# Attention scores as unsplit float32 blocks of 16 rows, four at a time, with two masked buffers

## The chip, the cores and the metric

The kernel runs on one core of a Trainium2 chip. The metric is the device time of one execution, in microseconds (us). The core has a matrix engine (TensorE, PE in the profile, with its weight loads as PEld), a vector engine (DVE), a scalar engine (ACT), GpSimd (POOL) and a queue that mostly issues DMAs (SP). Each engine runs its own list of instructions in order and waits at semaphores for the others. PSUM, where TensorE writes, has eight banks of 128 partitions x 512 float32.

## The reference, cut to what matters

The input `x` is (4, 2048, 256). All is float32.

```python
xn = _ln(q_x, ln1_w, ln1_b)                       # q_x is a plain layer norm of x
q = (xn @ wq + bq).reshape(b, n, H, HD).transpose(0, 2, 1, 3)   # H = 16 heads, HD = 16
k, v = ...                                        # likewise
fq = jax.nn.elu(q) + 1.0
fk = jax.nn.elu(k) + 1.0
kv = jnp.einsum('bhnd,bhne->bnde', fk, v)         # sums over the heads h, for each token n
qkv = jnp.einsum('bhnd,bnde->bhne', fq, kv)
qk = jnp.einsum('bhnd,bnd->bhn', fq, fk.sum(axis=1))
attn = qkv / (qk[..., None] + 1e-06)
x = q_x + attn_as_rows @ wo + bo
h = gelu(_ln(x, ln2_w, ln2_b) @ fc_w + fc_b)      # 256 -> 1024
y = x + (h @ proj_w + proj_b)
```

Around it stands `x = x + ...` and a second block: a layer norm, a gate from the mean over the sequence that picks two of eight experts for each batch, and for these gelu(x @ expert_w + expert_b), weighted and summed. The attention works inside one token: head h of a token meets the 16 heads of the same token. The kernel computes it as scores: for 8 tokens with 16 heads each, a 128 x 128 block of fk . fq, in which a mask keeps the entries of equal tokens; then masked scores times [v, 1] give qkv and qk together.

## The kernel before, in words

The 8192 tokens are cut into 16 tiles of 512. A tile passes through a software pipeline of named stages. `LAG` says how many iterations behind the newest tile a stage works, and the lists `FULL` and `HEAD` say in which order every engine walks the stages of an iteration; the order on each engine is thus written by hand. `walk` runs iterations 0 to 22: 2 has the attention rounds but no MLP, 3 to 6 have attention and MLP but no experts, 7 to 15 have all (7, 11 and 15 start from `HEAD`, with the gate G), 16 and 17 have no new tile, and the rest drains.

The stages that matter here:

- D2: v, q and k are xhT times w_qkv (L925, float32, 512 columns). ACT takes exp and relu of q and k (L517, L518), DVE joins them to elu + 1 (L696). Each feature is then split: ACT rounds it to float32r (L511, the high part), DVE subtracts (L689, the low part), and SP stores both parts to DRAM (L355).
- K0, K1: SP loads the features of one tile back (L381), head-major, half a tile each: 12 DMAs of 128 KB for each half. A block has 48 rows, three copies of the 16 features: high, low, high of k against high, high, low of q.
- B0, B9, and the B part of M1 to M4: the attention rounds, four to a tile (r = 0 to 3), of 16 blocks each. `scores` (L943) makes 8 blocks at a time in float32r, two row groups at once (partitions 0 to 47 and 64 to 111), into the banks ps0 and ps1. `masked` (L705, DVE) multiplies two banks with the mask into two of the four quarters of am. `weighted` (L952) multiplies am with vb into pt (32 columns each, four column groups at once), and ACT copies that to ot (L552). After rounds 1 and 3 SP stores ot and loads it back transposed as nd (L388, L393).
- N0, N: DVE divides (L737, L740) and splits the result (L747, L748). A2: times w_o (L1023), DVE adds and takes statistics (L758, L626), R: DVE normalises (L636). H: PE transposes (L876), ACT and DVE split into hT (L532, L728).
- C part of M1 to M4 and J7: the MLP. `up(m)`, m = 0 to 7, is six matmuls of 512 columns into pq0 or pq1 in turn (L980); ACT takes gelu twice (L545, L546), DVE subtracts (L721), `down(m)` is twelve matmuls of 256 columns into pj (L966).
- X and E: transposes of a new tile and of z. VL, VT: v loaded and transposed. F1, F3: the two experts (L888), F4: DVE joins them (L836), F2: transposes (L1069) and the last sum (L853).

PSUM: pt0, pt1 hold transposes, k and `weighted`; pq0, pq1 hold v, `up` and the experts; ps0, ps1 hold scores, q, A2 and E; pj0, pj1 hold `down` and F2. A round of PE stood as up(2r), weighted(r), half of the scores of round r+1, up(2r+1), the other half, down:

```python
for u in range(2):
    if "C" in parts:
        up(2 * r + u)
    if "B" in parts and u == 0:
        ...
        weighted(r)
    if "B" in parts and r < ROUNDS - 1:
        ...
        scores(r + 1, u)
```

## Time and profile before

| | |
|---|---|
| median of 3 runs | 1216.74 us (1216.59 to 1218.15) |
| the profiled execution's own time | 1216.43 us |
| its span | 1214.6 us |
| PE busy | 1066.1 us, 88% of the span |
| DVE busy | 791.8 us, 65% |
| ACT busy | 528.7 us, 44% |
| POOL busy | 184.0 us, 15% |
| DMA | 170.23 MB, of which the loads of kq and the stores of q and k are 84 MB |
| mean granted clock of TensorE | 0.912 of full speed |

The last row but one: 192 + 192 loads of 128.0 KB and 32 + 32 stores of 512.0 KB in the page's list of DMA issues. "Busy" of PE counts a matmul from its start to its modelled end, so overlapping matmuls count once and a full PE still may wait for weights. The duration of one instruction includes a fixed latency beside the time in which its data move. Rows of a timeline merge neighbours: start, length, engine, line, operation, output<-input, tile shape, count, and in brackets the idle time ahead and what ended it.

### The profile page before, as it was taken

What the parts mean: (1) busy time and instruction counts of PE and PEld (TensorE: products, weight loads), DVE (VectorE), ACT (ScalarE), POOL (GpSimd) and SP (SyncE); (2) the same over time, 40 slices, a digit from 0 to 9 for tenths busy, and PEclk for the clock granted to TensorE, in tenths of its full rate; (3) what the DMA queues carried; (4) which work ended last, traced back from release to release, by engine and by line L of the source; (5) the groups of instructions that cost most, each with busy time, mean ns of one, the idle gap of its engine ahead of it and who ended that gap; (6) DMA issues with size and microseconds to landing.
All of it is one profiled execution on the core that took longest, in us unless ns stands there. A gap on an engine that the chain in (4) does not pass through costs nothing.

```text
span 1214.6 us, 21887 instructions
## 1 busy us (share of the span) xinstructions
PE 1066.1 (88%) x7112; PEld 789.0 (65%) x7112; DVE 791.8 (65%) x1756; ACT 528.7 (44%) x835; POOL 184.0 (15%) x113
## 2 busy tenths in 40 slices
PE   5646988979798989999998899999999899796856
PEld 3334767767685858686776758686867667584623
DVE  2466576767666677768776676867687675656333
ACT  2414353635444443636364344636363444232322
POOL 1001111112111011211121111212112111202000
PEclk9858898979797989999997999999999899898969
DMA  4896948585857758676766658686767586321023
GB/s 169 172 189 135 170 105 174 109 176 107 173 112 160 146 127 181 150 171 142 178 132 169 138 131 174 146 183 147 172 139 177 130 174 140 84 56 62 21 76 108
DMA packets 331610, 170.23 MB, mean 140 GB/s; under 512 B 292752, under 2 KB 309392, under 8 KB 331280
## 3 DMA queue, kind: packets, MB, share of 16 engines
q1 hardware_dynamic: 324880, 158.81, 60.5%
q10 hardware_dynamic: 6656, 10.50, 2.5%
q8 instruction: 39, 0.64, 0.2%
q14 instruction: 35, 0.29, 0.1%
HBM read 93.75 MB, written 75.50 MB: 139 GB/s over the span
## 4 chain that ended last, share of the span: by engine, by line
PE 70%; issue 13%; DVE 9%; ACT 3%; POOL 2%; DMA 2%; SPq 0%; ACTq 0%; DVEq 0%; POOLq 0%
PE pq L980 15%; PE pj L966 13%; PE ps L943 10%; PE pq L888 9%; PE pt L952 5%; PE pq L925 4%; PE ps L925 3%; PE ps L1023 3%; PE pt L925 3%; PE pj L1069 2%; DVE am L705 2%; PE pt L876 2%; DVE acc L836 1%; DVE nd L737 1%; POOL x_sb L458 1%
## 5 line engine op out<-in xcount | busy, mean ns | idle before, releaser
L721 DVE TENSOR_TENSOR hidden<-xhT,hidden 128x512 fp32r<-128x512 f32 x128 | 88.5, 691 | 222.0 <-ACT hidden L546 221.4
L545 ACT ACTIVATE xhT<-pq,col 128x512 f32<-128x512 f32 x128 | 88.0, 688 | 324.5 <-PE pq L980 324.3
L980 PE MATMUL pq<-hT,w_fc 128*128 128x512 f32 x768 | 220.9, 426 | 4.8 <-issue 3.0
L966 PE MATMUL pj<-w_pj,hidden 128*128 128x256 f32 x1536 | 214.3, 289 | 2.7 <-DVE hidden L721 2.7
L966 PEld LDWEIGHTS pj<-w_pj,hidden 128*128 128x128 f32 x1536 | 191.6, 189 | 17.3 <-DVE hidden L721 3.7
L943 PE MATMUL ps<-kq 48*128 48x128 f32 x1024 | 155.3, 434 | 34.1 <-DVE am L705 19.7
L943 PEld LDWEIGHTS ps<-kq 48*128 48x128 f32 x1024 | 133.9, 330 | 75.1 <-issue 44.1
L705 DVE TENSOR_TENSOR am<-ps,mask 128x512 f32<-128x512 f32 x256 | 164.3, 683 | 26.1 <-PE ps L943 25.3
L980 PEld LDWEIGHTS pq<-hT,w_fc 128*128 128x128 f32 x768 | 147.3, 205 | 35.5 <-issue 4.7
L888 PE MATMUL pq<-zT,w_e 128*128 (+1 forms) x256 | 115.4, 604 | 7.9 <-DMA b_e<-in_eb 7.4
L552 ACT ACTIVATE ot<-pt,den_eps 128x512 f32<-128x512 f32 x64 | 78.9, 1233 | 31.6 <-PE pt L952 31.6
L888 PEld LDWEIGHTS pq<-zT,w_e 128*128 128x128 f32 x256 | 48.2, 193 | 63.6 <-issue 55.9
L546 ACT ACTIVATE hidden<-pq,col 128x512 fp32r<-128x512 f32 x128 | 87.0, 680 | 0.0
L952 PE MATMUL pt<-am,vb 128*32 128x128 f32 x2048 | 75.5, 292 | 5.8 <-DVE am L705 5.8
L455 POOL TENSOR_TENSOR x<-x,row 128x1024 f32<-128x1024 f32 x16 | 37.6, 2352 | 265.2 <-DVE x_sb L774 265.2
L952 PEld LDWEIGHTS pt<-am,vb 128*32 128x32 f32 x2048 | 56.8, 116 | 31.1 <-issue 30.7
L1023 PE MATMUL ps<-w_o,hT 128*128 128x256 f32 x384 | 56.4, 306 | 16.7 <-DVE hT L748 16.4
L925 PE MATMUL pq<-xhT,w_qkv 128*128 128x512 f32 x128 | 65.1, 656 | 2.5 <-ACT xhT L489 1.8
L1023 PEld LDWEIGHTS ps<-w_o,hT 128*128 128x128 f32 x384 | 50.4, 200 | 24.1 <-DVE hT L748 16.8
L737 DVE RECIPROCAL nd<-nd 128x256 f32<-128x256 f32 x32 | 55.9, 1748 | 14.4 <-DMA nd<-scratch_nd 14.4
L449 POOL TENSOR_TENSOR rs<-var,mhalf 128x8 f32 (+1 forms) x16 | 29.5, 1846 | 213.5 <-DVE var L651 208.2
L925 PE MATMUL pt<-xhT,w_qkv 128*128 128x512 f32 x128 | 57.5, 592 | 0.0
(114 smaller groups left out, 1298.4 us busy)
## 6 DMA issues: line engine op xcount, KB each, us to landing
kq<-scratch_q SPq DMA_DIRECT2D x192, 128.0 KB, 3.6
kq<-scratch_k SPq DMA_DIRECT2D x192, 128.0 KB, 4.5
scratch_q<-hidden SPq DMA_DIRECT2D x32, 512.0 KB, 4.6
scratch_k<-hidden SPq DMA_DIRECT2D x32, 512.0 KB, 6.1
scratch_nd<-ot SPq DMA_DIRECT2D x32, 512.0 KB, 4.4
nd<-scratch_nd SPq DMA_DIRECT2D x96, 128.0 KB, 2.6
x_sb<-in_x SPq DMA_DIRECT2D x16, 512.0 KB, 4.7
scratch_v<-feat_v ACTq DMA_DIRECT2D x16, 512.0 KB, 2.8
```

Of the source, the lines that this page charges most:

```text
L545: nc.scalar.activation(gelub[:, u], pq[u][:, :], ACT.Gelu, bias=b_fc[:, m:m + 1])
L546: nc.scalar.activation(hidden[:, m % SLOTS, 0], pq[u][:, :], ACT.Gelu, bias=b_fc[:, m:m + 1]).then_inc(S[f"pq_free{u}"], 1)
L552: nc.scalar.activation(dst[:, r // 2, RG * (r % 2):RG * (r % 2 + 1)], src, ACT.Identity, bias=den_eps[:, :]).then_inc(S[f"pt_free{r % 2}"], 1)
L705: nc.vector.tensor_tensor(am[:, 2 * b + h].rearrange("p (g n) -> p g n", n=P), ps[b][:, :].rearrange("p (g n) -> p g n", n=P), mask[:, :]. ...
L721: nc.vector.tensor_tensor(hidden[:, m % SLOTS, 1], gelub[:, u], hidden[:, m % SLOTS, 0].bitcast(f32), ALU.subtract).then_inc(S["rest_ready ...
L888: last = nc.tensor.matmul(pq[m][:, :], w[:, c, P * m:P * (m + 1)], zT[:, p.t % RING, c], start=(c == 0), stop=(c == NC - 1))
L925: last = nc.tensor.matmul(bank[:, :], w_qkv[:, j // NC, c, P * (j % NC):P * (j % NC + 1)], xhT[:, c], start=(c == 0), stop=(c == NC - 1))
L943: last = nc.tensor.matmul(ps[j // 2][:, P * g:P * (g + 1)], group(kd, j, g), group(qd, j, g), start=True, stop=True)
L952: last = nc.tensor.matmul(pt[r % 2][32 * j:32 * j + 32, P * g:P * (g + 1)], vb[:, GG * j + RG * r + g], am[:, j, P * g:P * (g + 1)], start ...
L966: last = nc.tensor.matmul(pj[u][:, D * s:D * (s + 1)], hidden[:, m % SLOTS, a, lo:lo + P], w_pj[:, b, m], start=(m == 0 and n == 0 and s = ...
L980: last = nc.tensor.matmul(pq[m % 2][:, :], w_fc[:, b, c, P * m:P * (m + 1)], hT[:, a, c], start=(n == 0), stop=(n == len(order) - 1))
L1023: last = nc.tensor.matmul(ps[u][:, D * s:D * (s + 1)], attnT[:, a, c, lo:lo + P], w_o[:, b, c], start=(c == 0 and n == 0), stop=(c == NC - ...
```

## The change

The features are no longer split. q and k features stay one float32 copy (`fqk`), stored and loaded once: K0 and K1 have 8 DMAs of 64 KB each. A block has 16 rows, and `scores(r)` makes all 16 blocks of a round in one piece, in plain float32, in four row groups (partitions 0, 32, 64, 96) and into four banks, which are one tensor ps of 128 x 4 x 512. `masked(r)` is then four DVE instructions behind one wait, into one of two buffers of am. B9 is gone; B0 makes round 0. In a round PE now runs scores(r+1) before weighted(r), with down(2r-1) and up(2r+1) between.

Since four banks belong to the scores, the others are shared anew: sa (ps 0, 1) holds X, v and A2; sb (ps 2, 3) holds q and E; pw0, pw1 hold k, VT, H, `up`, F1, G and `weighted`; pj also holds F3. `up(m)` uses pw1 for all m but 1, and `weighted` always pw0. K1 moves ahead of M4, VL ahead of M1, and B0 stands behind F4 and SA and ahead of H.

```diff
-FULL = ["L", "XS", "M1", "VL", "K0", "J2", "Y", "M2", "DS", "M3", "Z", "D1", "M4", "N0", "XL", "X", "J7", "JA", "YB", "E", "VT", "N", "D2", "K1", "A2",
-        "F1", "R", "F3", "B0", "F4", "SA", "H", "FX", "B9", "F2"]
+FULL = ["L", "XS", "VL", "M1", "K0", "J2", "Y", "M2", "DS", "M3", "Z", "D1", "K1", "M4", "N0", "XL", "X", "J7", "JA", "YB", "E", "VT", "N", "D2", "A2",
+        "F1", "R", "F3", "F4", "SA", "B0", "H", "FX", "F2"]
...
+        fqk = sb("fqk", [P, 2 * NC, T])
+        kq = sb("kq", [P, 2, 2, H * HALF])
...
-        am = sb("am", [P, 4, 512])
-        expb, relub = am[:, 0:2], am[:, 2:4]
+        am = sb("am", [P, 2, NQ, 512])
+        expb, relub = am[:, 1, 0:2], am[:, 1, 2:4]
...
-        pt = [ctx.enter_context(nc.psum_tensor(f"pt{n}", [P, 512], f32)) for n in range(2)]
-        pq = [ctx.enter_context(nc.psum_tensor(f"pq{n}", [P, 512], f32)) for n in range(2)]
-        ps = [ctx.enter_context(nc.psum_tensor(f"ps{n}", [P, 512], f32)) for n in range(2)]
+        ps = ctx.enter_context(nc.psum_tensor("ps", [P, NQ, 512], f32))
+        sa, sb2 = [ps[:, n] for n in range(2)], [ps[:, 2 + n] for n in range(2)]
+        pw = [ctx.enter_context(nc.psum_tensor(f"pw{n}", [P, 512], f32))[:, :] for n in range(2)]
...
+                    for n, dst in ((0, qd), (1, kd)):
+                        src = qk_dram[n][p.t % 2].rearrange("(j b) (d h) t -> j b d (h t)", b=2, h=H)
+                        for j in range(NQ):
+                            sp.dma_start(dst[32 * j:32 * j + HD, half], src[j, half]).then_inc(S[f"kq_in{half}"], 16)
...
-                        if j:
-                            rounded(j - 1)
-                    rounded(2 * NC - 1)
...
-                        if j:
-                            rest(j - 1)
-                    rest(2 * NC - 1)
...
+                def masked(r):
+
+                    wait("sc_full", at("sc_full", 1))
+                    wait("am_used", at("am_used"))
+                    for j in range(NQ):
+                        last = nc.vector.tensor_tensor(am[:, r % 2, j].rearrange("p (g n) -> p g n", n=P),
+                                                       ps[:, j].rearrange("p (g n) -> p g n", n=P),
+                                                       mask[:, :].unsqueeze(1).broadcast_to([P, RG, P]), ALU.mult)
+                    last.then_inc(S["sc_free"], 1)
...
+                def scores(r):
+
+                    wait("sc_free", at("sc_free"))
                     for g in range(RG):
-                        for j in (h, h + 2):
-                            last = nc.tensor.matmul(ps[j // 2][:, P * g:P * (g + 1)], group(kd, j, g), group(qd, j, g),
+                        at_g = slice(RG * (r % 2) + g, P * HG, HG)
+                        for j in range(NQ):
+                            rows = slice(32 * j, 32 * j + HD)
+                            last = nc.tensor.matmul(ps[:, j, P * g:P * (g + 1)], kd[rows, r // 2, at_g], qd[rows, r // 2, at_g],
                                                     start=True, stop=True)
...
+                    up_in_w = int("C" in parts and r == 0)
+                    if "C" in parts:
+                        up(2 * r)
+                        if r == 0:
+                            up(1)
+                    if "B" in parts and r < ROUNDS - 1:
+                        if r + 1 == ROUNDS // 2:
+                            wait("kq_in1", at("kq_in1"))
+                        scores(r + 1)
+                    if "C" in parts and r:
+                        wait("rest_ready", at("rest_ready"))
+                        down(2 * r - 1)
+                        up(2 * r + 1)
+                    if "B" in parts:
+                        weighted(r)
+                    if "C" in parts:
+                        wait("rest_ready", at("rest_ready", 1))
+                        down(2 * r)
```

Both kernels read the blocks with a step: `at_g`, and `group` before, take every eighth element (`HG` = 8), 128 of them.

How the instructions stand, first on PE, from A2 of iteration 2 into the second round of iteration 3. Before (L1023 is A2, L943 scores, L876 the transposes of H, L980 up, L952 weighted, L966 down):

```order
25 L1023 MATMUL ps<-w_o,hT 128x256 x24
26 L943 MATMUL ps<-kq 128x128 x8
27 L876 MATMUL pt<-ident,hn 128x128 x8
28 L943 MATMUL ps<-kq 128x128 x8
29 L980 MATMUL pq<-hT,w_fc 128x512 x6
30 L952 MATMUL pt<-am,vb 32x128 x16
31 L943 MATMUL ps<-kq 128x128 x8
32 L980 MATMUL pq<-hT,w_fc 128x512 x6
33 L943 MATMUL ps<-kq 128x128 x8
34 L966 MATMUL pj<-w_pj,hidden 128x256 x12
35 L980 MATMUL pq<-hT,w_fc 128x512 x6
36 L952 MATMUL pt<-am,vb 32x128 x16
```

And now (L1001 is A2, L920 scores, L858 H, L959 up, L930 weighted, L944 down):

```order
20 L1001 MATMUL ps<-w_o,hT 128x256 x24
21 L920 MATMUL ps<-kq 128x128 x16
22 L858 MATMUL pw<-ident,hn 128x128 x8
23 L959 MATMUL pw<-hT,w_fc 128x512 x12
24 L920 MATMUL ps<-kq 128x128 x16
25 L930 MATMUL pw<-am,vb 32x128 x16
26 L944 MATMUL pj<-w_pj,hidden 128x256 x12
27 L959 MATMUL pw<-hT,w_fc 128x512 x6
28 L920 MATMUL ps<-kq 128x128 x16
29 L944 MATMUL pj<-w_pj,hidden 128x256 x12
30 L959 MATMUL pw<-hT,w_fc 128x512 x6
31 L930 MATMUL pw<-am,vb 32x128 x16
```

The scores moved together into one piece of 16, and `weighted` moved from behind the first `up` of a round to behind the second.

On DVE, in the last part of iteration 15 and the start of 16, from the first expert to the first gelu rest. Before (L836 is F4, L728 the low part of H, L705 the masks, L853 the last sum, L721 the rest of a gelu; the body of the rarely taken branch is left out):

```order
609 L636 TENSOR_SCALAR hn<-x,mv,rs 128x256 x4
610 L705 TENSOR_TENSOR am<-ps,mask 128x512 x2
611 L836 SCALAR_TENSOR_TENSOR acc<-xhT,gtop,acc 128x512 x2
612 L728 TENSOR_TENSOR hT<-pt,hT 128x512 x2
...
626 L705 TENSOR_TENSOR am<-ps,mask 128x512 x2
627 L853 TENSOR_TENSOR out_sb<-pj,out_sb 128x512 x2
628 L721 TENSOR_TENSOR hidden<-xhT,hidden 128x512
```

And now (L817 is F4, L680 the masks, L710 the low part of H, L834 the last sum, L694 the rest of a gelu):

```order
549 L617 TENSOR_SCALAR hn<-x,mv,rs 128x256 x4
550 L817 SCALAR_TENSOR_TENSOR acc<-xhT,gtop,acc 128x512 x2
551 L680 TENSOR_TENSOR am<-ps,mask 128x512 x4
552 L710 TENSOR_TENSOR hT<-pw,hT 128x512 x2
...
566 L834 TENSOR_TENSOR out_sb<-pj,out_sb 128x512 x2
567 L694 TENSOR_TENSOR hidden<-xhT,hidden 128x512 x2
568 L680 TENSOR_TENSOR am<-ps,mask 128x512 x4
```

All four masks of round 0 now stand ahead of the low part of H, where two stood ahead of it and two behind.

## Rows read from the trace of the kernel before

**Rows 1.** Page, part 1: busy time of each engine, share of the span.

```profile
PE 1066.1 (88%) x7112; PEld 789.0 (65%) x7112; DVE 791.8 (65%) x1756; ACT 528.7 (44%) x835; POOL 184.0 (15%) x113
```

**Rows 2.** Page, part 4: the chain that ended last, by line.

```profile
PE pq L980 15%; PE pj L966 13%; PE ps L943 10%; PE pq L888 9%; PE pt L952 5%; PE pq L925 4%; PE ps L925 3%; PE ps L1023 3%; PE pt L925 3%; PE pj L1069 2%; DVE am L705 2%; PE pt L876 2%; DVE acc L836 1%; DVE nd L737 1%; POOL x_sb L458 1%
```

**Rows 3.** Windows: stretch, length, PE, PEld, DVE, ACT, POOL busy, granted clock, DMA, GB/s.

```profile
508.00:572.00 64.00, 63.27 (x441) 47.11 (x441) 48.17 (x104) 33.03 (x53) 11.60 (x6) 0.97 0.73 160
```

**Rows 4.** Timeline of PE in an iteration with all stages.

```profile
515.24 1.21 PE L943 MATMUL ps<-kq 48*128 48x128 f32 x8
...
517.92 1.22 PE L943 MATMUL ps<-kq 48*128 48x128 f32 x8 [0.45 <-DVE am L705]
...
521.00 2.08 PE L980 MATMUL pq<-hT,w_fc 128*128 128x512 f32 x6
...
526.87 1.21 PE L943 MATMUL ps<-kq 48*128 48x128 f32 x8
528.01 1.68 PE L966 MATMUL pj<-w_pj,hidden 128*128 128x256 f32 x12
529.53 1.57 PE L980 MATMUL pq<-hT,w_fc 128*128 128x512 f32 x6
...
538.85 1.57 PE L980 MATMUL pq<-hT,w_fc 128*128 128x512 f32 x6
...
548.18 1.57 PE L980 MATMUL pq<-hT,w_fc 128*128 128x512 f32 x6
549.68 1.08 PE L952 MATMUL pt<-am,vb 128*32 128x128 f32 x32
...
559.26 3.60 PE L925 MATMUL pq<-xhT,w_qkv 128*128 128x512 f32 x8
...
569.16 3.38 PE L1023 MATMUL ps<-w_o,hT 128*128 128x256 f32 x24
```

**Rows 5.** One line each, L943 at 541 us and at 187 us, weight loads: min/median/max ns.

```profile
L943 PEld LDWEIGHTS ps<-kq x8: 310/335/337, 541.4 to 542.1; 48*128 48x128 f32 x8
L943 PEld LDWEIGHTS ps<-kq x8: 308/335/337, 187.3 to 188.0; 48*128 48x128 f32 x8
```

**Rows 6.** The same view for other weight loads, all at full clock.

```profile
L952 PEld LDWEIGHTS pt<-am,vb x32: 106/110/110, 540.4 to 541.1; 128*32 128x32 f32 x32
L980 PEld LDWEIGHTS pq<-hT,w_fc x6: 187/188/189, 543.9 to 545.0; 128*128 128x128 f32 x6
L876 PEld LDWEIGHTS pt<-ident,xhat x8: 139/141/142, 554.9 to 555.7; 128*128 128x128 f32 x8
L933 PEld LDWEIGHTS pt<-ident,vd x8: 186/191/193, 558.3 to 559.0; 128*128 128x128 f32 x8
```

**Rows 7.** Timeline of DVE in the same iteration, around H.

```profile
516.48 1.29 DVE L705 TENSOR_TENSOR am<-ps,mask 128x512 f32<-128x512 f32 x2 [0.68 <-PE ps L943]
517.69 1.53 DVE L836 SCALAR_TENSOR_TENSOR acc<-xhT,gtop,acc 128x512 f32<-128x512 f32 x2
519.14 1.28 DVE L728 TENSOR_TENSOR hT<-pt,hT 128x512 fp32r<-128x512 f32 x2
```

**Rows 8.** Groups by line and shape: one of the two feature splits on DVE.

```profile
L689 DVE TENSOR_TENSOR hidden<-hn,hidden 128x512 fp32r<-128x512 f32 x32 | 22.0, 688 | 1.5
```

**Rows 9.** Timeline of PE in iteration 4, ahead of H.

```profile
249.14 1.97 PE L876 MATMUL pt<-ident,hn 128*128 128x128 f32 x8 [3.45 <-DVE hn L636]
```

**Rows 10.** Timeline of PE and DVE in iteration 2, one half round.

```profile
77.74 1.23 PE L943 MATMUL ps<-kq 48*128 48x128 f32 x8 [1.47 <-DVE am L705]
78.97 1.29 DVE L705 TENSOR_TENSOR am<-ps,mask 128x512 f32<-128x512 f32 x2 [1.38 <-PE ps L943]
```

**Rows 11.** The chain in order of time, iteration 16: start, length, what.

```profile
1021.72 1.27 ACT ot L552
...
1023.08 4.10 DMA scratch_nd<-ot
...
1037.84 4.42 PE ps L1023 x24
```

356 lines of the change are left out of this document (150 added, 206 removed), and 3 rows, old and new, of the table INC.

## The prediction

> **What bounds the kernel now.** I read the page first: PE is busy 88% of the span, DVE 65%, ACT 44% [rows 1], and the chain that ended last is PE nearly throughout, with the scores (L943) 10% of the span of it [rows 2]. So work taken off PE can count in full, and work taken off DVE, ACT or the DMA queue counts only where PE waits. Then the windows: in an iteration with all stages PE is busy 63.3 of 64 us at a granted clock of 0.97 [rows 3]; nothing but PE's list can shorten it. The timeline of PE there shows the only idle time, 0.45 us ahead of the second scores piece, behind DVE's masks, and an up of 2.08 us where others take 1.57, because the granted clock is half there [rows 4]. Earlier, in iterations 3 to 6 without experts, PE waits 3.45 us for DVE's norm ahead of H and goes on at half clock [rows 9]; in iteration 2 PE and DVE take turns, with 1.47 us of PE idle in each half round [rows 10]; in 16 and 17 the way from ot through DRAM to A2 is on the chain [rows 11].
>
> **The new scores piece.** This is the term on which all hangs: 16 blocks in one piece, of which the trace has no example. Before, 8 blocks are four pairs and take 1.14 us to the next instruction (526.87 to 528.01) [rows 4]; a round has two, 2.28 us. Now 16 blocks in four row groups are four sets, but float32 is two passes: where float32 is used before, the count shows it, 16 calls of L952 are 32 records [rows 4]. So it is eight sets of passes.
>
> What does a set cost? The trace says it is the weight load. In the old scores a load of 128 columns takes 335 ns, at full clock and at half clock alike [rows 5]; a load for `up`, also 128 columns, takes 188 and one of 32 columns 110 [rows 6]. From the last two: 0.81 ns a column, about 84 ns fixed. Then the scores' load moves data for 335 - 84 = 0.25 us, 2.4 times what `up` needs, and independent of the clock. Three readings fit:
> - The step. Scores read every eighth element. The transposes show the same: contiguous xhat 141 ns, the stepped vd 191 [rows 6], data time 57 against 107, nearly double. The new blocks keep the step, so a set stays at 0.25 us: the piece costs 1.14 for the first four sets and their start and end, plus 4 x 0.25 = 2.15 us, against 2.28 now. The part of the count that the row groups save is given back by the second pass.
> - Something in float32r or in 48 rows. Then float32 would run as L952 does, whose 32 records in four groups take 1.08 us [rows 4], and the piece is about 1.15.
> - The two row groups share one way in. Then four share it too, a set is 0.5 us and the piece 8 x 0.5 = 4.0.
>
> I take 2.15: the pair L876 and L933 is the nearest row that changes one thing only. The bounds for the range are 1.08, L952's own, and 4.0; less than L952 is excluded, since each pass streams 128 columns there too. The Trainium skill bears on this ("SBUF — State Buffer", section "Door 1: The DMA port swizzle (why `[64,N]` ≈ `[32,N]`)", its note on cachelines): consecutive accesses within 16 bytes run at full rate, each crossing to a new line pays. The trace agrees in the 141 against 191 ns; by it the piece is the 2.15 above.
>
> **One iteration with all stages** (7 to 15). Lengths from [rows 4]: up 1.5 (548.18 to 549.68), weighted 1.0, down 1.5 (528.01 to 529.53).
> - M1: before 8.53 (521.00 to 529.53), 0.5 of it slow clock. Now up, up, scores, weighted, down: 1.5 + 1.5 + 2.15 + 1.0 + 1.5 = 7.65, with the same 0.5 8.15: -0.4. `weighted(0)` must wait for the gelus of up(1) in the bank that they share: some 1.5 us after up(1); the scores between cover it.
> - M2, M3: before 9.32 each (529.53 to 538.85). Now 2 x 1.5 + 2.15 + 1.0 + 2 x 1.5 = 9.15: -0.15 each. up(2r+1) needs pw1 from up(2r), about 1.5 us after its end, behind 3.65 us of scores and down.
> - M4: the same work, but only down(5), 1.5 us, lies between up(6) and up(7) in one bank: +0.1.
> - From the end of F3 to up(0): before 5.76 (515.24 to 521.00). Now the piece ends 2.15 + 0.15 after F3; then DVE makes four masks (two are 1.29 [rows 7], four 2.5), and only then the low part of H, 1.28 [rows 7], for which up(0) waits. 2.3 + 2.5 + 1.3 + 0.15 = 6.25: +0.5. PE's transposes of H and F2 fit in between. Queued behind the masks on DVE are H, F2's sum and the first gelu rest; PE is who waits.
> - Round 3's ot comes later against the end of M4, since weighted(3) now stands behind up(7). From ot's start to A2 the way took 1.3 + 14.8 us in iteration 16 (1021.72 to 1037.84) [rows 11]. PE has, from weighted(3) to A2, the old 8.5 us up to D2 (550.76 to 559.26) less up and down, 5.5, and D2's 9.9 to 10.3 [rows 4], about 16; the way needs 0.5 + 16.1. The cover is thin: 0 to 0.7 us of wait, I take +0.25.
> Sum: -0.4 - 0.3 + 0.1 + 0.5 + 0.25 = +0.15, times 9: +1 us.
>
> **The other iterations.** 3 to 6: DVE loses the four subtractions of D2, 688 ns each [rows 8], of which one stood ahead of A2's sums: H moves forward by 0.7, and the masks that now stand ahead of its low part move it back by 0.3: -0.4. M1 to M4 give -0.4 - 0.3 + 0.1 = -0.6, and there is no wait at nd and no F3. -1.0 at most, I take -0.9: -3.5 for the four. Iteration 2: before, a round is twice 1.23 + 1.29 and a weighted at half clock, 1.9 (nearly twice the 1.08 of [rows 4]): 7.0 us [rows 10]. Now weighted runs beside DVE, since am has two buffers: 2.15 + 2.5 + 0.3 for two handovers = 4.95. Over four rounds -8; SP has fewer issues ahead of nd, so nothing there gives it back. 16 and 17: there no D2 covers the way through nd. M1 to M3 -0.7, F3 to up(0) +0.5 (once), weighted(3) later against M4's start by up and down, 3.0: +2.5 each, +5.
>
> What costs nothing: the loads of keys and the stores, halved; K1 ahead of M4 and VL ahead of M1 on SP, where the nd store of M4 now stands behind 8 issues of K1, which begin two rounds earlier; ACT's rounding. They gain nothing either, since PE waits for no DMA in [rows 3]. The fewer waits and switches of PE in a round I leave out.
>
> **Sum** against the profiled execution's own 1216.4 (span 1214.6), 0.3 under the median of the runs: +1 - 3.5 - 8 + 5 = -5.5. So 1211 us.
>
> **The rivals.**
> - *Fast loads* (the piece 1.15). Per iteration with all stages: M2, M3 -1.0 more each, M1 -0.6 (then the gelu of up(1) holds weighted(0)), F3 to up(0) -0.7 (then F4 holds the masks): -3.3 x 9 = -30; 3 to 6 -2.6 x 4 = -10; iteration 2 -3, 16 and 17 -6. 1211 - 49 = 1162. For it: L952 shows float32 with loads hidden in four column groups. Against: the step. The Trainium skill speaks for it ("TensorE: Matmul & The Clock Gate", Part 3, "Measured speedup vs the span model"): four row tiles ran 3.07 times as fast as one after the other; no run here shows it.
> - *Shared way* (the piece 4.0), slower. +1.85 for each of four pieces, 7.4 x 9 = +67; 3 to 6 three pieces, +22; iteration 2 +5, 16 and 17 +13: 1211 + 107 = 1318. For it: 0.25 is also twice 0.107 plus a little. Against: it needs a load of one row group to be as fast stepped as contiguous, which L933 beside L876 speaks against [rows 6]. It decides from a piece of about 2.3 us on.
> - *The idle time ahead of up(0) keeps the clock low*, slower. After the scores, H and F2 PE waits some 1.5 us at one place instead of 0.45 and crumbs. The granted clock is half there already for a part of up(0), 2.08 against 1.57 us [rows 4]; if the first up and half of the second run at half clock, that is 1.5 + 0.75 more instead of 0.5, +1.7 in each of 13 iterations, +22: 1233. Also longer waits at nd would look so.
> - *The fp32 blocks don't run in four groups at all*, that is the change doesn't do what it says: one after the other, worse than 4.0, and within the second rival's chance.
>
> **How the numbers follow.** Forecast 0.52, by itself 1201 to 1220; fast loads 0.22; shared way 0.12; clock 0.14. The 8 in 10: 1154 (the fast case with 8 us to spare) to 1236 (the clock case), leaving out the shared way and the ends. What a measurement can tell from no change is about 0.2%, 2.4 us. Faster: 0.33 of the forecast's 0.52, with 0.22: 0.55. Same: 0.12. Slower: 0.07 + 0.12 + 0.14 = 0.33.
>
> **What would show it.** In the profile after: the weight load of the scores near 335 ns and the piece 2.1 to 2.2 us for 32 records (forecast), or 190 and 1.1, or 500 and more and 4. F3's end to up(0) near 6.2 us with PE idle ended by DVE's low part of H. Rounds 2 and 3 of 9.1 to 9.2 us. A2 waiting under 0.7 us. Iteration 2's rounds near 5 us. The granted clock of 508 to 572 near 0.97; under 0.93 it is the clock case. I am wrong first of all if stepped float32 columns cost otherwise than stepped float32r ones.

## The result, and the profile after

The changed kernel takes 1195.89 us (median of 4 runs, 1193.74 to 1197.72) against 1216.66 us: ratio 0.9823, 95% interval 0.9807 to 0.9838. It is 20.8 us faster, where 5.5 were forecast; the direction and the range held, the size did not. Its profiled execution has a span of 1192.9 us against 1214.6, so the two traces differ by 21.7 us and can stand for the medians.

The page of the changed kernel, part 1, and the chain that ended last, by line, which answer to [rows 1] and [rows 2]:

```profile
PE 1048.4 (88%) x8136; PEld 779.5 (65%) x8136; DVE 729.8 (61%) x1692; ACT 499.5 (42%) x771; POOL 178.5 (15%) x113
...
PE pw L959 16%; PE pj L944 15%; PE ps L920 10%; PE ps L902 7%; PE pw L930 5%; PE pw L870 5%; PE pj L870 4%; PE pw L902 3%; DVE am L680 3%; PE ps L1001 3%; PE ps L858 2%; DVE hT L710 1%; POOL x_sb L447 1%; PE pw L910 1%; ACT hidden L526 1%
```

The scores (L920) are still 10% of the chain. They are 2048 records now instead of 1024, and each weight load took as long as before: 329 ns in the mean against 330 (the 335 of [rows 5] is a median; it is 333 now). The same kernel, groups by line and shape:

```profile
L920 PEld LDWEIGHTS ps<-kq 16*128 16x128 f32 x2048 | 128.5, 329 | 42.3 <-issue 33.3 <-DVE am L680 9.1
```

The timeline of PE in an iteration with all stages, and DVE around H, which answer to [rows 4] and [rows 7]:

```profile
494.21 2.29 PE L920 MATMUL ps<-kq 16*128 16x128 f32 x32
496.43 1.09 PE L858 MATMUL pw<-ident,hn 128*128 128x128 f32 x8
...
500.56 3.06 PE L959 MATMUL pw<-hT,w_fc 128*128 128x512 f32 x12 [2.16 <-DVE hT L710]
503.54 2.29 PE L920 MATMUL ps<-kq 16*128 16x128 f32 x32
505.77 1.08 PE L930 MATMUL pw<-am,vb 128*32 128x128 f32 x32
...
508.31 1.56 PE L959 MATMUL pw<-hT,w_fc 128*128 128x512 f32 x6
...
517.60 1.56 PE L959 MATMUL pw<-hT,w_fc 128*128 128x512 f32 x6
...
526.86 1.57 PE L959 MATMUL pw<-hT,w_fc 128*128 128x512 f32 x6
...
548.00 3.38 PE L1001 MATMUL ps<-w_o,hT 128*128 128x256 f32 x24
```

```profile
496.57 2.48 DVE L680 TENSOR_TENSOR am<-ps,mask 128x512 f32<-128x512 f32 x4 [0.64 <-PE ps L920]
498.97 1.28 DVE L710 TENSOR_TENSOR hT<-pw,hT 128x512 fp32r<-128x512 f32 x2
```

A piece of 16 blocks takes 2.23 us (503.54 to 505.77). From F3's end to up(0) pass 6.35 us (494.21 to 500.56), 2.16 of them idle behind the low part of H. Rounds 2 and 3 take 9.29 and 9.26 us. A2 follows D2 without a wait. The window of this iteration, to hold against [rows 3] (PE 63.27 of 64.00 us, clock 0.97, DMA 0.73):

```profile
500.56:564.52 63.96, 61.74 (x504) 45.94 (x505) 43.28 (x100) 31.17 (x48) 11.06 (x6) 1.00 0.44 111
```

**Where the 21.7 us are.** I divided both traces at the start of up(0) of each iteration. Each stretch is the time between two such starts, so the sum is the whole.

| stretch | before | after | difference | forecast |
|---|---|---|---|---|
| start to up(0) of iteration 3 | 126.5 | 117.5 | -9.0 | -8 |
| iterations 3 to 6 | 256.6 | 246.1 | -10.5 | -3.5 |
| 7 to 15 | 608.7 | 604.2 | -4.5 | +1 |
| 16 and 17 | 124.4 | 126.2 | +1.8 | +5 |
| the rest | 98.4 | 98.9 | +0.5 | 0 |

Iterations 5 and 6 show the largest difference, 3.7 us each. Iteration 5 took 65.3 us before (252.5 to 317.8) and 61.6 after (240.4 to 302.0). Its last part, from A2 to up(0), first before, then after, from the timelines of PE:

```profile
304.13 3.38 PE L1023 MATMUL ps<-w_o,hT 128*128 128x256 f32 x24
309.77 1.22 PE L943 MATMUL ps<-kq 48*128 48x128 f32 x8 [2.26 <-DVE x L758]
314.43 1.96 PE L876 MATMUL pt<-ident,hn 128*128 128x128 f32 x8 [3.44 <-DVE hn L636]
...
317.81 1.65 PE L980 MATMUL pq<-hT,w_fc 128*128 128x512 f32 x3 [0.26 <-DVE hT L728]
```

```profile
289.43 3.38 PE L1001 MATMUL ps<-w_o,hT 128*128 128x256 f32 x24
293.87 2.30 PE L920 MATMUL ps<-kq 16*128 16x128 f32 x32 [1.07 <-DVE x L740]
298.34 1.97 PE L858 MATMUL pw<-ident,hn 128*128 128x128 f32 x8 [2.17 <-DVE hn L617]
302.02 1.21 PE L959 MATMUL pw<-hT,w_fc 128*128 128x512 f32 x2 [1.72 <-DVE hT L710]
```

From A2 to H 10.30 us became 8.91, from H to up(0) 3.38 became 3.68. The first part of the same iteration held two more differences. The timeline of PE before, at its first and second round:

```profile
260.32 1.21 PE L943 MATMUL ps<-kq 48*128 48x128 f32 x8 [0.98 <-DVE am L705]
...
263.31 2.76 PE L980 MATMUL pq<-hT,w_fc 128*128 128x512 f32 x6
```

The wait of 0.98 us for masks is gone after. So is the up of 2.76 us, which ran nearly all at half the granted clock (others take 1.57). In all, the three rounds before M4 take 27.9 us after (240.42 to 268.32) and took 30.6 (252.52 to 283.15). The two windows of the iteration, before and after, say the same of the granted clock, the third number from the right, 0.89 and 0.92:

```profile
252.50:317.80 65.30, 58.35 (x416) 45.07 (x416) 44.94 (x98) 30.34 (x47) 11.30 (x6) 0.89 0.68 141
```

```profile
240.40:302.00 61.60, 56.62 (x480) 44.12 (x480) 39.52 (x93) 28.47 (x43) 10.75 (x6) 0.92 0.39 98
```

### The profile page after: what moved, and what is told of

The parts are those of the page before. It is cut to its first block, busy times and chain, and to the rows that moved or that the text cites. A ratio compares the mean times of both kernels' runs of the same rounds, so it can differ in the third digit from the quotient of the medians.

```text
span 1192.9 us, 23418 instructions
## 1 busy us (share of the span) xinstructions
PE 1048.4 (88%) x8136; PEld 779.5 (65%) x8136; DVE 729.8 (61%) x1692; ACT 499.5 (42%) x771; POOL 178.5 (15%) x113
## 4 chain that ended last, share of the span: by engine, by line
PE 72%; issue 11%; DVE 9%; POOL 2%; DMA 2%; ACT 2%; DVEq 0%; SPq 0%; ACTq 0%; POOLq 0%
PE pw L959 16%; PE pj L944 15%; PE ps L920 10%; PE ps L902 7%; PE pw L930 5%; PE pw L870 5%; PE pj L870 4%; PE pw L902 3%; DVE am L680 3%; PE ps L1001 3%; PE ps L858 2%; DVE hT L710 1%; POOL x_sb L447 1%; PE pw L910 1%; ACT hidden L526 1%
## 5 line engine op out<-in xcount | busy, mean ns | idle before, releaser
L959 PE MATMUL pw<-hT,w_fc 128*128 128x512 f32 x768 | 212.1, 417 | 30.4 <-DVE hT L710 29.7
L944 PE MATMUL pj<-w_pj,hidden 128*128 128x256 f32 x1536 | 214.1, 289 | 1.4 <-DVE hidden L694 1.4
L694 DVE TENSOR_TENSOR hidden<-xhT,hidden 128x512 fp32r<-128x512 f32 x128 | 88.6, 692 | 201.1 <-ACT hidden L526 201.1
L944 PEld LDWEIGHTS pj<-w_pj,hidden 128*128 128x128 f32 x1536 | 192.3, 189 | 22.5 <-issue 14.9
L525 ACT ACTIVATE xhT<-pw,col 128x512 f32<-128x512 f32 x128 | 88.1, 688 | 279.9 <-PE pw L959 279.3
L959 PEld LDWEIGHTS pw<-hT,w_fc 128*128 128x128 f32 x768 | 144.5, 199 | 66.1 <-DVE hT L710 31.7
L680 DVE TENSOR_TENSOR am<-ps,mask 128x512 f32<-128x512 f32 x256 | 158.9, 684 | 17.6 <-PE ps L920 17.5
L920 PE MATMUL ps<-kq 16*128 16x128 f32 x2048 | 146.9, 438 | 16.0 <-DVE am L680 9.2
L920 PEld LDWEIGHTS ps<-kq 16*128 16x128 f32 x2048 | 128.5, 329 | 42.3 <-issue 33.3
L902 PE MATMUL ps<-xhT,w_qkv 128*128 128x512 f32 x256 | 120.6, 627 | 2.5 <-ACT xhT L478 2.5
L532 ACT ACTIVATE ot<-pw,den_eps 128x512 f32<-128x512 f32 x64 | 81.8, 1278 | 49.6 <-PE pw L930 49.6
L719 DVE RECIPROCAL nd<-nd 128x256 f32<-128x256 f32 x32 | 56.0, 1749 | 60.2 <-DMA nd<-scratch_nd 60.2
L902 PEld LDWEIGHTS ps<-xhT,w_qkv 128*128 128x128 f32 x256 | 51.0, 205 | 61.6 <-issue 58.4
L526 ACT ACTIVATE hidden<-pw,col 128x512 fp32r<-128x512 f32 x128 | 87.2, 681 | 0.0
L1001 PE MATMUL ps<-w_o,hT 128*128 128x256 f32 x384 | 57.0, 308 | 21.2 <-DVE hT L730 21.2
L930 PE MATMUL pw<-am,vb 128*32 128x128 f32 x2048 | 73.0, 286 | 1.9 <-ACT ot L532 1.4
L930 PEld LDWEIGHTS pw<-am,vb 128*32 128x32 f32 x2048 | 54.6, 113 | 23.2 <-issue 16.4
L1001 PEld LDWEIGHTS ps<-w_o,hT 128*128 128x128 f32 x384 | 51.0, 203 | 28.7 <-DVE hT L730 21.6
L870 PE MATMUL pw<-zT,w_e 128*128 (+1 forms) x128 | 59.9, 612 | 7.2 <-DMA b_e<-in_eb 7.2
```

The lines of the kernel that those rows point to most:

```text
L525: nc.scalar.activation(gelub[:, m % 2], pw[n], ACT.Gelu, bias=b_fc[:, m:m + 1])
L526: nc.scalar.activation(hidden[:, m % SLOTS, 0], pw[n], ACT.Gelu, bias=b_fc[:, m:m + 1]).then_inc(S[f"pw_free{n}"], 1)
L532: nc.scalar.activation(dst[:, r // 2, RG * (r % 2):RG * (r % 2 + 1)], src, ACT.Identity, bias=den_eps[:, :]).then_inc(S["pw_free0"], 1)
L680: last = nc.vector.tensor_tensor(am[:, r % 2, j].rearrange("p (g n) -> p g n", n=P), ps[:, j].rearrange("p (g n) -> p g n", n=P), mask[:, ...
L694: nc.vector.tensor_tensor(hidden[:, m % SLOTS, 1], gelub[:, u], hidden[:, m % SLOTS, 0].bitcast(f32), ALU.subtract).then_inc(S["rest_ready ...
L870: last = nc.tensor.matmul(bank, w[:, c, P * m:P * (m + 1)], zT[:, p.t % RING, c], start=(c == 0), stop=(c == NC - 1))
```

## The experiments

Each comparison is with the kernel before, run beside it on the same chip (median 1217.5 to 1218.3 us). The changed kernel stands at 0.9823.

### What sets the piece: the step or the row groups

`blocks_contiguous`, `keys_contiguous`, `step_of_two` and `step_of_four` change only the slices that the blocks of the changed kernel read, and the blocks then mix other tokens and heads. `keys_contiguous` does it for the keys alone. This is `blocks_contiguous`:

```diff
-                        at_g = slice(RG * (r % 2) + g, P * HG, HG)
+                        at_g = slice(P * (RG * (r % 2) + g), P * (RG * (r % 2) + g + 1))
```

> The changed kernel, but each block of the scores reads 128 neighbouring elements of the keys and queries instead of every eighth, so the blocks mix other tokens and heads; everything else stands. My theory, the step of eight in the read of the weights sets the piece of 16 blocks at 2.23 us: the weight load falls from 329 ns to 190 or less and the piece to 1.1 to 1.3 us. Rounds 2 and 3 then fall from 9.27 to about 8.3 us, and the kernel to 1145 to 1160 us from 1196. Rival, the piece is set by float32 with 16 rows in four row groups, not by the step: load 329 ns, piece 2.2 us, 1196 us. A third case is that the weight load falls but the piece stays near 2 us, then streaming 128 columns at 128 partitions of output in each of eight sets is the limit.

> The changed kernel, but only the stationary operand of the scores (the keys) is read as 128 neighbouring elements, the moving one (the queries) still with the step of eight; the blocks are then not the reference's. If the step costs in the weight load alone, this is as fast as with both contiguous: load 190 ns or less, piece 1.1 to 1.3 us. If the stepped moving read has a price of its own, the piece lies between that and 2.2 us; if only the moving read costs, it stays 2.2 us with a load of 329 ns or less.

> The changed kernel, but the blocks read every second element of keys and queries instead of every eighth, so they mix other tokens and heads. With a step of eight the piece took 2.23 us and the weight load 329 ns, with neighbours 1.10 us and 195 ns. If what costs is each jump to another 16 bytes, a step of two halves the jumps: the piece comes near 1.1 to 1.4 us. If any step but one costs in full, it stays 2.2 us with a load of 329 ns. Only in the first case is a layout that puts 16 tokens of a head together worth its smaller DMA pieces.

> The changed kernel with the blocks of the scores reading every fourth element, mixing other tokens and heads. Measured so far: step one 1.10 us a piece, two 1.16, eight 2.23; keys in neighbours and queries with step eight 2.05. If the cost goes with the 16 bytes that are touched, a step of four touches as many as one of eight and takes 2.2 us. If it grows with the distance, it lies between, near 1.5 us.

`row_group_after_group` computes the same and turns the loops over:

```diff
-                    for g in range(RG):
-                        at_g = slice(RG * (r % 2) + g, P * HG, HG)
-                        for j in range(NQ):
+                    for j in range(NQ):
+                        for g in range(RG):
+                            at_g = slice(RG * (r % 2) + g, P * HG, HG)
```

> The changed kernel with the 16 blocks of a piece in another order: all four blocks of a row group one after the other, then the next row group; the result is the same. If the four row groups work at the same time in the changed kernel (my reading of 2.23 us: eight sets at 0.25 us and a start), neighbours now share a row group and the piece takes 5 us or more, up to 32 x 0.33 = 10.6 us, 12 to 35 us more in each iteration. If the groups share one way in for the weights and never overlapped, the order does not matter: 2.2 us and 1196 us.

| blocks read | weight load | piece | kernel |
|---|---|---|---|
| step 8 (the change) | 329 ns | 2.23 us | 1195.9, ratio 0.9823 |
| step 4 | 324 | 2.19 | 1197.1 (one run) |
| step 2 | 202 | 1.16 | 1155.9 (one run) |
| neighbours | 195 | 1.10 | 1152.5, ratio 0.9464 (0.9445 to 0.9482) |
| keys neighbours, queries step 8 | 205 | 2.05 | 1191.4 (one run) |
| step 8, one row group after the other | 329 | 5.66 | 1485.8 (one run) |

The time of a piece is taken from its first record to the next instruction of PE. The weight loads in the groups by shape, of `blocks_contiguous`, `keys_contiguous`, `step_of_two` and `step_of_four`; the mean of one instruction is the second number behind the first bar:

```profile
L920 PEld LDWEIGHTS ps<-kq 16*128 16x128 f32 x2048 | 66.6, 195 | 42.6 <-issue 33.3 <-DVE am L680 9.3
```

```profile
L921 PEld LDWEIGHTS ps<-kq 16*128 16x128 f32 x2048 | 106.9, 205 | 46.2 <-issue 34.7 <-DVE am L680 9.1
```

```profile
L922 PEld LDWEIGHTS ps<-kq 16*128 16x128 f32 x2048 | 70.6, 202 | 43.2 <-issue 33.9 <-DVE am L680 9.3
```

```profile
L922 PEld LDWEIGHTS ps<-kq 16*128 16x128 f32 x2048 | 126.3, 324 | 42.2 <-issue 33.1 <-DVE am L680 9.1
```

So the step sets the piece, and the four row groups do work at the same time: one after the other they cost 2.5 times as much. (The granted clock of that run is 0.827 in the mean, so its kernel time is not the price of the piece alone.) But `keys_contiguous` corrects the theory. PE in its timeline:

```profile
503.63 2.12 PE L921 MATMUL ps<-kq 16*128 16x128 f32 x32
505.68 1.08 PE L931 MATMUL pw<-am,vb 128*32 128x128 f32 x32
```

With the keys as neighbours the weight load is 205 ns and the piece is still 2.05 us. So the moving operand, read with a step, holds a set of passes to about 0.25 us by itself (2.05 / 8), and undoing the keys' step gives back 0.18 of the 1.13 us that both steps cost. The opposite case, queries as neighbours and keys with the step, was not run, so it is not shown that the load alone would cost anything. The nearest rows speak against it. They are the transposes of [rows 6], in which only the loaded operand is stepped (vd, L933) or none is (L876), in the timeline of the kernel before:

```profile
557.50 1.04 PE L876 MATMUL ps<-ident,hn 128*128 128x128 f32 x8
558.38 1.05 PE L933 MATMUL pt<-ident,vd 128*128 128x128 f32 x8
559.26 3.60 PE L925 MATMUL pq<-xhT,w_qkv 128*128 128x512 f32 x8
```

The eight records take 0.88 us in both, though a load takes 191 ns in one and 141 in the other.

The price is no slope: between two and four it jumps and after that stands still, so it does not follow the distance. The Trainium skill has a rule that fits ("SBUF — State Buffer", section "Specifications (TRN2)"): the memory works in lines of 16 bytes and wants at least two hits in each for full rate. With four bytes an element, step two has two hits and step four has one; the trace agrees, with 1.16 and 2.19 us.

`old_blocks_contiguous` does the same to the kernel before.

```diff
-                        return src[64 * (j // 2):64 * (j // 2) + KP, r // 2, lo + RG * (r % 2) + g:lo + P * HG:HG]
+                        lo += P * (RG * (r % 2) + g)
+                        return src[64 * (j // 2):64 * (j // 2) + KP, r // 2, lo:lo + P]
```

> The kernel before, but the blocks read 128 neighbouring elements of keys and queries instead of every eighth; the blocks mix other tokens and heads. If the step sets the weight load, it falls from 335 ns to about 190 (as the load of L980, also 128 columns of float32r) and 8 blocks from 1.14 us to 0.6 to 0.75; six to eight such pieces lie on the path of PE in an iteration with all stages, -3 to -4 us each, about 1170 to 1185 us instead of 1216.7. If something in float32r with 48 rows in two row groups sets it, the load stays 335 ns and the time 1216.7.

The load fell to 206 ns, 8 blocks from 1.14 to 0.59 us and the kernel to 1182.5 us, ratio 0.9717 (0.9690 to 0.9744). Type and rows stayed as they were, so the price was nothing in float32r or in 48 rows.

### The masks ahead of the low part of H

```diff
-        "F1", "R", "F3", "F4", "SA", "B0", "H", "FX", "F2"]
+        "F1", "R", "F3", "F4", "SA", "H", "B0", "FX", "F2"]
```

> The changed kernel with B0 moved behind H in both orders, so PE transposes H before it makes the scores of round 0, and DVE makes the low part of H before the four masks. My theory, up(0) waits for the masks ahead of the low part of H: F3's end to up(0) falls from 6.35 us to 0.93 (H) + 2.23 (scores) + 0.93 (F2) = 4.1, with no idle time of PE ended by the low part of H: -2.2 in each of the nine iterations with experts and in 16 and 17, -0.4 in 3 to 6 (3.68 to 3.3 from H to up(0)): about -26, 1170 us. Rival, the wait comes back later: the masks now end 2.2 us later against up(0), and scores(1) or weighted(0) waits for them, then M1 grows from 7.75 to 9 or 10 us and the kernel stays within 5 us of 1196.

1174.8 us, ratio 0.9654 (0.9637 to 0.9670). PE in the same iteration of `h_before_masks`:

```profile
496.85 1.04 PE L858 MATMUL pw<-ident,hn 128*128 128x128 f32 x8
497.82 2.29 PE L920 MATMUL ps<-kq 16*128 16x128 f32 x32
...
500.89 3.04 PE L959 MATMUL pw<-hT,w_fc 128*128 128x512 f32 x12
```

4.04 us instead of 6.35 and no idle time: H's work on ACT and DVE passes behind the scores. The masks came in time for scores(1), so the wait did not return. An iteration with all stages is 61.5 us, of which PE is busy 61.4. Against the change it is -21 us, where -26 were expected. `h_before_masks_late` keeps B0 ahead of H in iterations 2 to 6.

> The changed kernel with B0 behind H only from iteration 7 on, where the experts cover the norm, and ahead of H in iterations 2 to 6, as in the change. Behind H everywhere it took 1174.8 us, but iterations 4 to 6 took 62.0 to 62.3 us there against 61.6 in the changed kernel, and the first up(0) came at 119.4 instead of 117.5 us. Theory: both are kept, 3 to 4 us less than with H first everywhere: 1171 us. Rival, the earlier up(0) is lost again where the order changes between iterations 6 and 7, or as half clock: 1175 us.

1173.1 us, 0.9631 (0.9612 to 0.9649). Iterations 5 and 6 did fall from 62.0 to 61.6 us, but the two intervals overlap, and the first up(0) came at 119.6 us, not 117.5: the timing does not tell the two apart.

`old_masks_together` puts B9 ahead of H in the kernel before.

> The kernel before with B9 moved ahead of H, so that all masks of round 0 stand ahead of the low part of H, as in the change; one part of the change alone, the result is the same. Theory: in iterations 4 to 6 the wait of 0.98 us of PE for masks in the first round goes (all are done before up(0)), and the stretch of half clock behind it (262.6 and 327.4 us) with it: -2 to -2.5, less 0.5 for a later up(0), so iterations 5 and 6 fall from 65.3 to about 63.3 us. Rival, the half clock there comes from elsewhere: then only 0.5 is gained and 64.8 us stand. In iterations with experts up(0) comes 0.5 to 0.9 us later than before (5.76 from F3's end becomes 6.3 to 6.7), so the whole kernel moves by -3 to +5 us in the theory, +3 to +8 in the rival.

This missed: 1237.8 us, ratio 1.0158 (1.0141 to 1.0175). I had forgotten the banks. B0 and B9 use the same two, so with nothing between them PE stood idle 1.47 us for the first masks in an iteration with all stages, and in iterations 4 to 6 another 1.41 us ahead of up(0), behind the low part of H (0.26 before). As it stands in the change, the move rests on the four banks. It also leaves open what makes the stretch of half clock behind the first round: iterations 4 and 6 had it (67.6 and 67.7 us), 5 had not (66.1).

### Transfers

`doubled_feature_transfers` stores and loads the features twice.

> The changed kernel with every store of q and k features made twice (the second into a tensor that nobody reads) and every load of them made twice (the second into rows that nobody reads): +33.6 MB, two thirds of the DMA bytes that the change saved, and the issues on SP doubled. Theory: the transfers cost and gain nothing, since PE waits for none of them: 1196 within 2 us. Rival, part of the 15 us that the forecast missed is relief of the DMA engines: then nd comes later again and 5 to 10 us come back.

1203.2 us, ratio 0.9892 (0.9855 to 0.9929), some 7 us slower than the change. The size is the rival's, the place is not. Iterations 5 to 15 take what they took without it, to 0.1 us. The first up(0) comes at 123.0 instead of 117.5 us, since in iteration 2 PE waits 4.11 us ahead of A2 (108.48 us), behind the way through nd; iterations 3 and 4 add 1.6. In the kernel before, with more bytes still, the wait ahead of that A2 was 0.30 us. So the gain over the kernel before is no relief of the DMA engines. But the changed kernel needs what it saved: with two thirds of the bytes back it would have gained 15 us instead of 21.

What weighs in iteration 2 is the issues on SP, not the bytes. K1 stands ahead of M4 on SP now, and with it ahead of the store of round 3's ot. The store in SP's timelines, first of the changed kernel, then of `doubled_feature_transfers`:

```profile
91.69 0.55 SPq L377 DMA_DIRECT2D scratch_nd<-ot  x1
```

```profile
95.71 0.55 SPq L380 DMA_DIRECT2D scratch_nd<-ot  x1
```

ACT finishes ot at 89.54 and 89.74 us. The 8 issues of K1 then end at 91.65, the 16 at 95.67, and the store follows. It lands 4.1 us after its issue in both. So already in the change K1 holds this store for 2 us, which the wait ahead of A2 does not show yet; K1's earlier place is free only as long as it is 8 issues.

### The multiplications of the attention

Of the 64 DVE multiplications L740, 47 take 0.42 us, 8 take 2.57 and the others lie between. All the long ones run beside GpSimd's sums; DVE and GpSimd before, in iteration 8:

```profile
498.57 2.91 DVE L740 TENSOR_TENSOR nd<-nd 128x256 f32<-128x256 f32 x2
```

```profile
498.60 2.60 POOL L458 TENSOR_TENSOR x_sb<-x_sb,row 128x1024 f32 x1
```

`old_without_bias_add` shrinks GpSimd's sum to one column:

```diff
-                    nc.gpsimd.tensor_tensor(slot, slot, rows_of(D), ALU.add).then_inc(S["pool_chain"], 1)
+                    nc.gpsimd.tensor_tensor(slot[:, :, 0:1], slot[:, :, 0:1], rows_of(D)[:, :, 0:1], ALU.add).then_inc(S["pool_chain"], 1)
```

> The kernel before, in which GpSimd's second sum of stage YB (L458, the bias that is added to x_sb) covers one column of 256 instead of all, so 255 columns miss that bias. It takes away the work that runs beside DVE's multiplications of the attention (L740), one of which takes 2.57 us instead of 0.42 in most iterations. Theory: that is a collision of the two engines; without it the mean of L740 falls from 825 ns to about 420 to 550, the way from ot to A2 in iterations 16 and 17 shortens by 1.5 us each, and in 3 to 6 the first elu comes up to 1 us earlier: -4 to -6 us, about 1211. Rival, the slow multiplications wait for their data and not for GpSimd: 825 ns as before, 1216.7.

1213.3 us, ratio 0.9954 (0.9938 to 0.9970), and L740's mean fell from 825 to 471 ns. The collision costs about 5 us before. In the changed kernel it does not happen (L722, 422 ns each): the reciprocals wait longer for nd (60.2 us in all instead of 14.4), and the multiplications so come after GpSimd's pair. The Trainium skill names a mechanism ("SBUF — State Buffer", section "🔬 SBUF: two separate sides"): a DVE instruction with two inputs in SBUF and a GpSimd instruction that reads SBUF share one pair of ports, which the one that starts first holds to its end. The trace agrees: the second multiplication above starts behind the sum and ends at 501.48, 0.28 us after it, and the sums that begin while a multiplication runs take 2.53 to 2.60 us, the others 2.34 to 2.35.

### The work of the split

`old_without_low_part` cuts the four subtractions (L689) of the kernel before to one column from the second tile on, `old_without_split` also the four roundings on ACT (L511):

```diff
+                        n = T if isinstance(p.t, int) and p.t == 0 else 1
-                        nc.scalar.activation(hidden[:, j, 0], src, ACT.Identity).then_inc(S["hi_ready"], 1)
+                        nc.scalar.activation(hidden[:, j, 0, 0:n], src[:, 0:n], ACT.Identity).then_inc(S["hi_ready"], 1)
```

> The kernel before, in which the four subtractions on DVE that make the low part of the features (L689) cover one column instead of 512 from the second tile on, so the low parts that the keys and queries take are stale. It takes one part of the change alone. Theory: in iterations 3 to 6 two of the four subtractions stand between the last elu and A2's sums, so the sums, the norm and H come 1.3 to 1.4 us earlier: -1.3 in each of the four, -5 in all, and nothing where experts stand behind A2; about 1211. Rival from the forecast, one of them counts: -0.6 each, -2.5. Rival, they are hidden everywhere: 1216.7 within 1 us.

> The kernel before, in which from the second tile on both halves of the split of the features, ACT's four roundings (L511) and DVE's four subtractions (L689), cover one column instead of 512, so keys and queries take stale parts. With the subtractions alone gone, the time fell by 1.9 us only. Theory: the roundings stand between the exps on ACT and hold the last elu and A2's sums as much as the subtractions do; with both gone the way from A2 to H in iterations 3 to 6 falls from 10.3 us to about 8.9, as in the changed kernel: -1.3 in each of four, -2 in iteration 2, so -6 to -8 us against before. Rival, the wait is set by the late multiplications of the attention ahead of D2 on DVE: then no more than -3.

Without the subtractions 1216.2 us, 0.9987 (0.9975 to 1.0000), -1.9: less than the expected -5, and hardly clear of no change. Without both 1205.8 us, 0.9881 (0.9851 to 0.9911), -12: more than expected. ACT and DVE of the kernel before in iteration 5 show how the two hang together:

```profile
304.52 0.63 ACT L511 ACTIVATE hidden<-xhat 128x512 fp32r<-128x512 f32 x1
305.04 0.69 ACT L517 ACTIVATE am<-pt,col 128x512 f32<-128x512 f32 x1
305.61 0.69 ACT L518 ACTIVATE am<-pt,col 128x512 f32<-128x512 f32 x1
```

```profile
306.34 0.69 DVE L696 SCALAR_TENSOR_TENSOR hn<-am 128x512 f32<-128x512 f32 x1 [0.38 <-ACT am L518]
306.95 1.48 DVE L689 TENSOR_TENSOR hidden<-hn,hidden 128x512 fp32r<-128x512 f32 x2
308.34 1.28 DVE L758 TENSOR_TENSOR x<-x,ps 128x512 f32<-128x512 f32 x2
```

DVE waits for ACT's last relu, and ACT makes that only after the roundings between its exps; then two subtractions, not one, stand ahead of A2's sums (L758). In `old_without_split` A2 to up(0) of iteration 5 is 12.4 us instead of 13.7, and the stretch of half clock in its first rounds is gone, another 1.5. The roundings alone were not taken out, so their part is known only as what comes on top of the subtractions: 10 of the 12 us.

`split_work_put_back` is the reverse: the changed kernel with roundings and subtractions that nobody uses.

> The changed kernel with the work of the split put back where it stood, without its use: ACT rounds each feature into hidden (four of some 0.65 us), DVE subtracts (four of 0.69 us); keys and queries are stored whole as in the change, and the result is the same. Taking that work out of the kernel before gained 12 us. Theory, most of the 15 us that the forecast missed is that work: A2 to up(0) in iterations 3 to 6 goes from 12.6 back to about 13.9 us, iteration 2's from 13.3 to 14.5, and some stretches of half clock come back in iterations 5 and 6: +7 to +12 us, 1203 to 1208. Rival, it is hidden in the changed kernel, because the multiplications of the attention are no longer slow there: 1196 to 1199.

1211.7 us (median of 10), ratio 0.9942 (0.9923 to 0.9961), some 15 us slower than the change and more than the expected 7 to 12. A2 to H of iteration 5 in its timeline of PE is 10.8 us, where the change has 8.91:

```profile
302.11 3.38 PE L1015 MATMUL ps<-w_o,hT 128*128 128x256 f32 x24
308.47 2.30 PE L934 MATMUL ps<-kq 16*128 16x128 f32 x32 [2.98 <-DVE x L754]
312.93 1.96 PE L872 MATMUL pw<-ident,hn 128*128 128x128 f32 x8 [2.16 <-DVE hn L624]
```

Its profiled execution is the slowest of the ten, with a span of 1213.1 us. Divided as above, of the 20.2 us by which that is over the changed kernel's, 5.3 lie ahead of the first up(0), 12.3 in iterations 3 to 6 and 3.3 in 7 to 15. L736, the multiplication, stays at 421 ns, so the collision has no part in it.

### A whole version without the costly step

To keep the groups of tokens and have a step of two, the features must lie differently. `tokens_in_sixteens` starts from `h_before_masks_late`. ACT writes exp and relu in another order, every fourth token next to each other. So 16 tokens of a head lie side by side, and the stores go in pieces of 64 B:

```diff
-                        nc.scalar.activation(expb[:, j % 2], bank[:, :], ACT.Exp, bias=b_qkv[:, j:j + 1])
+                        src, e, rl = (x.rearrange(f"p (u {o})  -> p u w G", w=TA * STEP, G=HG // STEP) for x, o in
+                                      ((bank[:, :], "w G"), (expb[:, j % 2], "G w"), (relub[:, j % 2], "G w")))
+                        nc.scalar.activation(e, src, ACT.Exp, bias=b_qkv[:, j:j + 1])
...
-                        at_g = slice(RG * (r % 2) + g, P * HG, HG)
+                        i = RG * (r % 2) + g
+                        lo = STEP * P * (i % (HG // STEP)) + i // (HG // STEP)
+                        at_g = slice(lo, lo + STEP * (P - 1) + 1, STEP)
```

`tokens_in_eights` is the same with STEP 1. `sixteens_read_permuted` only walks the tokens in the other order (`p u G w`), so that ACT's read of PSUM is stepped and its write is not.

> A version meant to be right and faster: h_before_masks_late with another layout of the features. ACT writes exp and relu in another order of the tokens (fourth and fourth together), so that 16 tokens of a head lie side by side; SP stores pieces of 64 B and loads pieces of 1 KB, and each block reads every second element. The groups of tokens, v and ot stay as they are. Theory: as with a step of two the piece takes about 1.15 us instead of 2.23, -40 us at most as 1155.9 against 1195.9: 1130 to 1140 us. Rivals: ACT's scattered writes or the smaller pieces (+150 thousand packets) cost back: if the stores take over twice 2.7 us, keys come late and PE waits at kq, 1150 us or more; if the norm chain in the iterations without experts is then the bound, 1140 to 1150.

> The same with 8 tokens of a head side by side: each block is then 128 neighbouring elements, the stores go in pieces of 32 B and the loads in pieces of 512 B. Against the sixteens it gains what the step of two still costs, 299 against 293 ns a matmul, about 3 us of the whole, and pays with 262 thousand more packets. Theory: the DMA engines, busy some 40% now, take that, 1128 to 1138 us. Rival: packets cost the same whatever their size, the stores take 10 us or more and PE waits for keys: 1150 us or more.

> tokens_in_sixteens with one thing changed: ACT walks through the tokens in the order in which they are written, so it reads the PSUM bank with a step of four elements and writes exp and relu to neighbouring places, instead of reading neighbours and writing with a step of 16. In tokens_in_sixteens exp and relu took 1.14 us each instead of 0.69, and the first up(0) came at 123.4 us instead of 117.5 to 119.6; A2 to up(0) in iterations without experts took 13.6 to 14.6 instead of 12.6 us. If it is the scattered write that costs, exp and relu come back to about 0.69 us and 5 to 9 us are gained: 1131 to 1135 us from 1139.7. If a walk over three dimensions costs whichever side is scattered, 1.14 us stay, and 1140.

| | kernel | ratio | exp on ACT | store of q |
|---|---|---|---|---|
| sixteens | 1139.7 us | 0.9350 (0.9315 to 0.9385) | 1.13 to 1.15 us | 5.8 us |
| eights | 1184.2 | 0.9727 (0.9687 to 0.9767) | 1.18 to 1.24 | 11.4 |
| sixteens, read permuted | 1132.4 | 0.9285 (0.9254 to 0.9315) | 0.69 | 5.7 |

The groups of ACT in `tokens_in_sixteens` and in `sixteens_read_permuted`:

```profile
L509 ACT ACTIVATE am<-pw,col 128x512 f32<-128x512 f32 x32 | 36.8, 1150 | 4.9 <-DVE fqk L680 4.9
```

```profile
L509 ACT ACTIVATE am<-pw,col 128x512 f32<-128x512 f32 x32 | 22.0, 688 | 18.3 <-DVE fqk L680 12.9 <-PE pw L910 5.2
```

The write with a step of 64 bytes cost ACT 0.45 us each time; the stepped read of PSUM costs nothing measurable (exp takes 688 ns in the changed kernel too). The eights missed the expected 1128 to 1138 us by 46 and came as their rival said. They pay for their small pieces: the packets of SP's queue take 78.8% of the 16 engines' span instead of 45.3%, and PE waits 7.17 us ahead of A2 in iteration 2. `sixteens_read_permuted` leaves nothing out and takes 1132.4 us, 85 us less than the kernel before beside it.

## Why the prediction was right or wrong, step by step

- **The piece, 2.15 us:** measured 2.23, and the step is the reason, as forecast. The two rival readings were refuted by the chip: neighbours in float32r run fast too, and the row groups overlap. But the way by which the step costs was read wrongly. I had it in the weight load alone; without the load's step the piece is still 2.05 us, so the moving operand holds it, which stood in no term. The rows on which I rested it, L933 beside L876, show longer loads but passes that follow each other just as fast. The number came out by luck, since the moving operand's limit of about 0.25 us a set is the one that I had read off the loads.
- **An iteration with all stages, +0.15:** M2 and M3 forecast 9.15, measured 9.29 and 9.26; F3's end to up(0) 6.25, measured 6.35, with the idle time ended where I had said. M4 grew by 0.3 (+0.1 forecast, 7.18 after against 6.87 in iteration 9). M1 took 7.75 us (500.56 to 508.31): the 0.5 us of slow clock that I had left in it was gone. The wait at nd that I gave +0.25 did not come. Iteration 8 took 64.0 us against 63.7, iteration 9 64.0 against 64.1; that the sum is so near is in part these misses taking each other off.
- **Iteration 2, -8:** -9.0 to up(0) of iteration 3. A round is 4.90 us (forecast 4.95) against 7.23 before (I had 7.0), but the last one ends with waits for ACT, and all that lies ahead of A2 gave -6.8 (104.23 instead of 111.01 us). The other -2.2 came from A2 to up(0), 13.3 us instead of 15.5. I had no term for it; it is 15.6 again with the split's work put back. So the number held in part by luck. The timeline of PE after, one round:

```profile
75.89 2.30 PE L920 MATMUL ps<-kq 16*128 16x128 f32 x32 [0.90 <-DVE am L680]
...
80.79 2.30 PE L920 MATMUL ps<-kq 16*128 16x128 f32 x32 [0.73 <-DVE am L680]
```

- **Iterations 3 to 6, -3.5: this term failed.** It was -10.5. The step that failed is the sentence "What costs nothing: ... ACT's rounding", and with it "-0.4" for H. I priced the subtractions at 2.8 us in all (four times 0.7), and the run without them gained 1.9. I priced at nothing the four roundings, which hold the relus for which DVE waits. The runs put the split's work, both together, at 12 us in the kernel before and some 15 in the changed one, most of it in iterations 2 to 6. The three parts of iteration 5: 1.39 us from A2 to H less 0.30 for the masks (forecast 0.7 less 0.3), 0.98 us of wait in the first round, which I had in no row and did not look for, and about 1.5 us of half clock.
- **7 to 15, +1:** -4.5: -4.1 in the iterations 7, 11 and 15 that begin with HEAD, -1.7 in iteration 10, +1.0 in 14. In iteration 11 all of it is the first round, 11.4 us before and 9.7 after, at a higher granted clock. I had taken one iteration for all nine, and the clock as given: by the reckoning below it gave 10 us here. So without the clock the nine iterations became some 6 us longer (an estimate, 10 less 4.5), not 1.
- **16 and 17, +5:** +1.8. That weighted(3) comes later against A2 held: up(0) to ot 32.2 us after, 29.9 before, +2.3. But the way from ot to A2 shortened from 16.12 to 14.67 us. The chain after, in order of time, which answers to [rows 11]:

```profile
1000.04 1.24 ACT ot L532
...
1001.29 4.09 DMA scratch_nd<-ot
...
1011.91 0.77 DVE nd L722 x2
...
1014.71 4.93 PE ps L1001 x24
```

The multiplications take 0.77 us there and took 2.30: the collision, 1.5 us in each of the two iterations. `old_without_bias_add` took 3.8 us off these two in the kernel before. I had taken the way's length of [rows 11] as fixed.
- **The clock rival, +22:** it went the other way. The mean granted clock is 0.928 instead of 0.912. That is 171 us at half clock instead of 215 (twice the missing share of the span), 31 instead of 63 in iterations 7 to 15 and 41 instead of 52 in 3 to 6. To price it I took the intervals from one matmul to the next without a wait, and compared those at half clock with the median of the same two lines at full clock. At half clock they are 62 us longer in all before and 50 after. The figure is rough: with intervals up to 0.6 us alone it is 55 and 42. So the clock gave some 12 of the 21.7 us, more than half, 10 of them in 7 to 15, 5 in 3 to 6 and 2 in 16 and 17, less 4.5 ahead of the first up(0). Putting the split's work back raises the price from 50 to 61, so in the changed kernel most of it is a consequence of the shorter waits, as I read it. Taking that work out of the kernel before lowered it only from 62 to 61. What decides on one stretch, such as that at 262 us, I can't say.

The wrong size is therefore two terms: an engine's work called free because PE waits for no instruction of it by name, and one iteration, with its granted clock, read for several.

## What to carry to other kernels

Ask of work that is taken off a helper engine not only whether PE waits for it, but whether the instruction for which PE does wait stands behind it, on its own engine or on the one that feeds it. Read the operands' step before the number of rows or the type: in these small float32 matmuls a step of four or more elements in both operands doubled the price, undoing it for the loaded one alone gave back 0.18 of 1.13 us, and undoing it for both gave all. And when a piece grows on an engine, put the short work for which the bound engine waits ahead of it, if other work covers the long one.

## What the runs showed of the hardware that I had not expected

- The step costs in the moving operand: 2.05 us with it alone stepped, 2.23 with both, 1.10 with none. Between steps of two and four elements lies nearly the whole price (1.16 and 2.19 us). A stepped load alone lengthened the loads of the transposes from 141 to 191 ns and not their pace, 0.88 us for eight records.
- The weight load of stepped operands takes the same 330 ns for 16 rows in float32 as for 48 in float32r, and with neighbours 195 and 206 ns.
- A DVE multiplication of 0.42 us takes up to 2.57 beside a GpSimd sum, and the sum 2.53 to 2.60 instead of 2.35 where it begins during a multiplication.
- ACT reads PSUM with a step of four elements at full speed (688 ns for 512 columns) and writes with a step of 16 elements at 1140.
- Stores of q, 256 KB in pieces of 256, 64 and 32 B, land in 2.7, 5.8 and 11.4 us (median from issue to landing).
- 16 issues of loads on SP took 8.1 us and 8 took 4.6, and the store behind them was issued only at their end, with its own 4.1 us to landing unchanged.
